# Expert second stage sub-tile by sub-tile, slot table ahead of the tile table, first dummy adds left out

## What is computed

```
x = x + 0.5 * ffn(layernorm(x)); x = x + attn(layernorm(x)); x = x + 0.5 * ffn(layernorm(x))

ffn (T = 8192 tokens, 8 experts, 2 of them a token, cap = 2560 rows an expert, F = 1024):
logits = clip(xf @ Wr); top_v, top_i = top_k(logits, 2); top_p = softmax of the two
pos = rank of a token among those of its expert; kept = pos < cap
xe = rows of xf gathered by expert and rank
h = silu(xe @ W1) * (xe @ W3); ye = h @ W2
out[token] += top_p * kept * ye
```

## Time and profile before

| | us |
|---|---|
| timed runs, median of 3 | 3054.07 |
| timed runs, lowest and highest | 3050.84, 3055.57 |
| profiled execution, its time | 3048.99 |
| profiled execution, its span | 3047.3 |
| TensorE busy | 2854.6 (94%) |
| DVE busy | 1602.6 (53%) |
| ACT busy | 1253.7 (41%) |
| POOL busy | 1158.8 (38%) |

### The profile page before, as it was taken

One profiled execution on the slowest core, in us unless ns is written; L12 is line 12 of the kernel. 1 busy time (PEld: TensorE's weight loads), 2 busy tenths in 40 slices (PEclk: granted clock), 3 DMA queues, 4 the chain that ended last, 5 costly groups with the idle time before them and its releaser, 6 DMA issues. The chain is left out here.

```text
span 3047.3 us, 54514 instructions
## 1 busy us (share of the span) xinstructions
PE 2854.6 (94%) x18727; PEld 2543.1 (83%) x18727; DVE 1602.6 (53%) x3791; ACT 1253.7 (41%) x2685; POOL 1158.8 (38%) x1560
## 2 busy tenths in 40 slices
PE   5379999999999999979999994999999999999997
PEld 3368898989899988868888884898998998898986
DVE  8843544454454545347778775345545454445443
ACT  5233434344444434334444442344434343444433
POOL 3654444444443434310111123443434443444432
PEclk9689999999999999989999996999999999999999
DMA  7542323232323312220111013323323232323221
GB/s 251 177 119 39 80 36 77 42 77 42 77 44 75 84 30 41 36 54 29 58 56 59 30 44 95 85 40 76 77 43 77 42 81 32 80 42 77 41 36 26
DMA packets 156550, 198.51 MB, mean 65 GB/s; under 512 B 15696, under 2 KB 128464, under 8 KB 156368
## 3 DMA queue, kind: packets, MB, share of 16 engines
q0 software_dynamic: 64128, 88.42, 17.6%
q1 hardware_dynamic: 81952, 97.30, 9.8%
q10 hardware_dynamic: 10288, 10.38, 1.0%
HBM read 124.32 MB, written 80.11 MB: 67 GB/s over the span
## 5 line engine op out<-in xcount | busy, mean ns | idle before, releaser
L1259 DVE TENSOR_TENSOR e_h_lo<-e_hid,e_h_hi 128x384 fp32r<-128x384 f32 (+1 forms) x640 | 383.7, 600 | 399.2 <-ACT e_h_hi L1219 399.2
L1256 DVE TENSOR_TENSOR e_hid<-e_ps,e_gate 128x384 f32<-128x384 f32 (+1 forms) x640 | 382.0, 597 | 308.4 <-ACT e_gate L1215 308.3
L1219 ACT ACTIVATE e_h_hi<-e_hid 128x384 fp32r<-128x384 f32 (+1 forms) x640 | 356.7, 557 | 444.1 <-DVE e_hid L1256 443.8
L1215 ACT ACTIVATE e_gate<-e_ps 128x384 f32<-128x384 f32 (+1 forms) x640 | 333.5, 521 | 330.7 <-PE e_ps L101 330.5
L99 PE MATMUL e_ps<-e_xT_hi,c_wa 128*128 128x384 f32 (+1 forms) x1280 | 454.5, 355 | 9.0 <-DVE e_yrow L1269 6.0
L99 PE MATMUL e_ps<-e_xT_hi,e_wb 128*128 128x384 f32 (+1 forms) x1280 | 460.3, 360 | 0.0
L100 PE MATMUL e_ps<-e_xT_lo,e_wb 128*128 128x384 f32 (+1 forms) x1280 | 455.1, 356 | 0.0
L101 PE MATMUL e_ps<-e_xT_hi,e_wb 128*128 128x384 f32 (+1 forms) x1280 | 455.0, 355 | 0.0
L101 PE MATMUL e_ps<-e_xT_hi,c_wa 128*128 128x384 f32 (+1 forms) x1280 | 449.7, 351 | 0.0
L100 PE MATMUL e_ps<-e_xT_lo,c_wa 128*128 128x384 f32 (+1 forms) x1280 | 449.7, 351 | 0.0
L433 POOL DMA_INDIRECT c_xrow<-normed_rows,e_token x320 | 347.8, 1087 | 156.6 <-issue 91.3
(11 more groups left out here) (297 smaller groups left out, 5189.5 us busy)
## 6 DMA issues: line engine op xcount, KB each, us to landing
c_raw<-w SPq DMA_DIRECT2D x204, 256.0 KB, 5.5
normed_rows<-r_xn SPq DMA_DIRECT2D x8, 1056.0 KB, 7.2
normed_rows<-mi_xn SPq DMA_DIRECT2D x8, 1056.0 KB, 4.7
x<-x ACTq DMA_DIRECT2D x8, 1024.0 KB, 12.3
out<-mi_x SPq DMA_DIRECT2D x8, 1024.0 KB, 5.3
r_xin<-x SPq DMA_DIRECT2D x7, 1024.0 KB, 11.0
c_raw<-x SPq DMA_DIRECT2D x7, 1024.0 KB, 8.1
c_xrow<-normed_rows,e_token POOLq DMA_INDIRECT x320
```

The costliest lines, as they stand in the source:

```text
L1215: act.activation(gate[:, f % 2, 0:n], ps1[f % 2][:, 0:n], ACT.Silu).then_inc(gated, 1)
L1219: act.activation(h[0][:, f, 0:n], hid[:, f % 2, 0:n], ACT.Copy).then_inc(h_high, 1)
L1256: dve.tensor_tensor(hid[:, f % 2, 0:n], ps3[f % 2][:, 0:n], gate[:, f % 2, 0:n], ALU.mult).then_inc(hid_ready, 1)
L1259: dve.tensor_tensor(h[1][:, f, 0:n], hid[:, f % 2, 0:n], h[0][:, f, 0:n].bitcast(F32), ALU.subtract).then_inc(h_ready, 1)
```

## The change

1. `Router.tiles` is cut in two: `read_counts` (its first instruction, which frees the PSUM bank) stays where it was, and `read_table` now goes ahead of the rest, in the route phase ahead of `low_w` too.
2. The second stage on TensorE runs by sub-tile: 0 and 2 for f = 0 to 6, both for f = 7, then 3 (in a big tile), then 1. `y_made` and `y_kept` go up at each sub-tile, ACT and DVE take the sub-tiles in that order, and `y_lent_kept` is gone: slice 1 of the next tile waits for all but the last sub-tile of this one.
3. On POOL `meta(g + 1)` goes behind the adds of iteration g and ahead of its gather, and waits for the landing of those adds. The first expert's first tile sends no adds (its code is written out in front of the loop), and the single dummy add is gone.
4. The last tile's adds are issued one by one as their sub-tiles are kept.
5. The first turn of a phase takes three sub-tiles instead of four, and the two splits of x behind it 384 columns instead of 512.
6. The loads of x1's groups 1 and 2 go from the end of e1_ to SP's start in the middle phase.

```diff
-    def tiles(self, dve, table):
+    def read_counts(self, dve):
+        dve.wait_ge(self.count_made, 1)
+        dve.tensor_scalar(self.lg[:, 0, :], self.rank_bank[...], float(CAP), float(P - 1), ALU.min, ALU.add)
...
-                r.tiles(dve, tiles_out)
+                r.read_counts(dve)
+                dve.wait_ge(r.tabled, T // P // QUAD)
+                r.read_table(dve, r.table_bank[:, 0:SCOLS], slot_token)
                 for q in range(LOW_BY_POOL, PIECES):
                     low_w(q)
-                dve.wait_ge(r.tabled, T // P // QUAD)
-                r.read_table(dve, r.table_bank[:, 0:SCOLS], slot_token)
+                r.tiles(dve, tiles_out)
...
-                def tile(e, subs, at, behind, g):
-                    meta(g)
+                def tile(e, subs, at, behind, g, adds=True):
                     hold(e, subs, at, g)
-                    wait_alone(pool, y_kept, g + 1, k.passed)
-                    add(BIG)
+                    if adds:
+                        wait_alone(pool, y_kept, BIG * g + BIG, k.passed)
+                        add(range(BIG))
+                    meta(g + 1, adds)
                     gather(behind, g)
...
-                wait_alone(pool, held, 1, k.passed)
-                add(1)
-                with pool.Fori(0, E) as e:
+                meta(0, False)
+                expert(0, adds=False)
+                with pool.Fori(1, E) as e:
                     expert(e)
...
-                wait_alone(pool, y_kept, n + 2, k.passed)
-                add(SMALL)
+                for sub, kept in zip(RESULTS[SMALL], (1, BIG - 1, BIG)):
+                    wait_alone(pool, y_kept, BIG * n + BIG + kept, k.passed)
+                    add((sub,))
...
                         if f == 1:
-                            pe.wait_ge(y_lent_kept, g + 1)
+                            pe.wait_ge(y_kept, BIG * g + 2 * BIG - 1)
...
+                    for f in range(KF - 1):
+                        second(f, 2)
+                    pe.wait_ge(h_ready, KF * g + KF)
+                    for sub in (0, 2):
+                        second(KF - 1, sub).then_inc(y_made, 1)
...
-        for g in (1, 2):
-            sp.dma_start(x1[:, g], x1_g[g]).then_inc(self.x_loaded[g], 16)
...
+                load(1)
+                load(2)
                 for g in range(MGS):
```

More of the change, by code:

```diff
@@ L44 @@
 MAX_BIG, MAX_SMALL, MAX_TILES = 3, 4, 6
+RESULTS = {SMALL: (0, 2, 1), BIG: (0, 2, 3, 1)}
 TAIL = 2 * BIG
@@ L377, in count @@
         pe.matmul(self.rank_bank[:, self.RANK_AT:self.RANK_AT + E], self.k.ones[:], self.seen[:], start=True, stop=True).then_inc(self.count_made, 1)
+    def read_counts(self, dve):
+        dve.wait_ge(self.count_made, 1)
+        dve.tensor_scalar(self.lg[:, 0, :], self.rank_bank[:, self.RANK_AT:self.RANK_AT + E], float(CAP), float(P - 1),
+                          ALU.min, ALU.add).then_inc(self.count_read, 1)
     def tiles(self, dve, table):
@@ L385, in tiles @@
         scan, zero, count = self.lg[:, 2, :], self.lg[:, 3, :], self.lg[:, 4, :]
-        dve.wait_ge(self.count_made, 1)
-        dve.tensor_scalar(units, self.rank_bank[:, self.RANK_AT:self.RANK_AT + E], float(CAP), float(P - 1), ALU.min,
-                          ALU.add).then_inc(self.count_read, 1)
         dve.memset(zero, 0.0)
@@ L1058, in add @@
                 def add(subs):
-                    for sub in range(subs):
+                    for sub in subs:
                         pool.indirect_dma_start(
@@ L1063, in add, with meta @@
                             compute_op=ALU.add).then_inc(y_added, 16)
-                def meta(g):
-                    pool.wait_ge(y_added, WORDS * g + 16)
+                def meta(g, adds):
+                    if adds:
+                        pool.wait_ge(y_added, WORDS * g - WORDS)
                     wait_alone(pool, held, g + 1, k.passed)
@@ L1141, in _, with turn @@
                 pe.nop().then_inc(y_made, 1)
-                def turn(n_loaded):
+                def turn(n_loaded, subs=BIG):
                     pe.wait_ge(x_loaded, n_loaded)
                     for half in range(KD):
-                        for sub in range(BIG):
+                        for sub in range(subs):
                             ins = pe.transpose(psx[:, half, sub * P:(sub + 1) * P],
@@ L1156, in wt, with second @@
                         return both[:, 0, at:at + P], both[:, 1, at:at + P]
-                    def second(f, of):
+                    def second(f, sub):
                         at = W2AT + f * D
-                        for sub in of:
-                            own, bank = slice(sub * P, (sub + 1) * P), ybank[sub]
-                            pe.matmul(bank[:].rearrange("p (u d) -> p u d", u=2), h[0][:, f, own],
-                                      both[:, :, at:at + D], start=(f == 0), stop=False)
-                            ins = pe.matmul(bank[:, D:2 * D], h[1][:, f, own], both[:, 0, at:at + D],
-                                            start=False, stop=(f == KF - 1))
-                        return ins
+                        own, bank = slice(sub * P, (sub + 1) * P), ybank[sub]
+                        pe.matmul(bank[:].rearrange("p (u d) -> p u d", u=2), h[0][:, f, own],
+                                  both[:, :, at:at + D], start=(f == 0), stop=False)
+                        return pe.matmul(bank[:, D:2 * D], h[1][:, f, own], both[:, 0, at:at + D],
+                                         start=False, stop=(f == KF - 1))
                     if first:
@@ L1266, in tile @@
                             low_w(e, s, q)
-                    for i, sub in enumerate(reversed(range(subs))):
+                    for i, sub in enumerate(RESULTS[subs]):
                         dve.wait_ge(y_scaled, BIG * g + i + 1)
```

65 lines of the change are left out of this document (31 added, 34 removed).

## The result

| | before | after |
|---|---|---|
| timed runs, median (4 runs each) | 3054.82 us | 3001.07 us |
| lowest and highest | 3050.84, 3055.69 | 2999.50, 3001.51 |
| profiled execution, its time | 3048.99 | 2999.50 |
| profiled execution, its span | 3047.3 | 2997.8 |

The ratio is 0.9826, with a 95% interval of 0.9809 to 0.9843. The two profiled executions are 49.5 us apart. The other 4.3 lie in the base: the profiled execution of before was 5.8 us faster than the median of its runs, that of after 1.6. In the later experiments before had medians of 3051.6 to 3052.3 us, and beside 3051.63 the unchanged after took 3000.85, 50.8 less; the first four runs of before were somewhat slow.

What follows compares the result with a forecast made beforehand. TensorE was taken as short of work only at the expert phases' starts and the seams between phases. Terms 12.2 + 9.1 + 1.4 + 3.4 + 2.5 + 6.8 + 1.4 = 36.8 us off 3054.07 gave 3017, range 3009 to 3031.

Steps and rivals of the forecast that it cites:

- The starts: Stalls at the first tiles of both expert phases vanish: 9.1 us in the first, 12.2 in the second; first turns add 1.4.
- The seam from the middle phase: Ahead of the second expert phase, DVE's tile table runs while POOL issues the gather, saving 3.4 us.
- No stretch below a granted clock of 1.00: Sign of being right: at the first expert phase's start, no granted clock below 1 in 200 to 220 us.
- no pair slower: Second-stage matmul pairs on TensorE keep 0.346 us each; slower pairs would have shown the one-bank rival.
- Rivals (a) to (d): Tile 0 waits for dummy adds (0.12); one-bank pairs slow (0.04); landing binds every tile (0.03); dummies not holding gather (0.03).
- The first turn: In both expert phases, six transposes for eight and narrower copies save 0.7 us each, 1.4 together.
- The step that failed: In steady tiles, finishing results earlier gains 0 for the next tile's slice 1, since no steady tile waited there.
- The first seam: From routing to the first expert phase, earlier slot table, weight loads and gather save 2.5 us, bounds 1.2 and 4.0.
- SP ends last then: At the first seam SP's weight loads end last, at 155.2, 1.2 us sooner, hiding the table of tiles.
- The gather beside DVE's splits: At the first seam the gather's issue may take up to 1.4 us longer beside DVE's splits, under SP's cover.
- The ends: At both expert phases' ends, adding sub-tiles singly saves 3.9 us less some waits between adds: 3.4 each, 6.8 together.
- x1's loads: At the seam to the middle phase, SP issues two x1 loads less before the barrier, saving 1.4 us.

Runs made afterwards that it cites:

- run 8: The kernel after, with SP's twelve loads of the second expert's weights moved behind the barrier into the first expert phase; 2997.29 us, ratio 0.9823.
- run 2: The kernel before with only POOL's part (part 3) of the change, the last three adds still together; 3028.42 us, ratio 0.9928.
- run 3: The kernel before with only read_counts, the slot table first and x1's two loads behind the barrier; 3043.19 us, ratio 0.9974.
- run 5: The kernel after with two useless ACT copies ahead of the first gate of each expert's first tile; 3006.33 us.
- run 9: The kernel after with two useless DVE instructions behind the last addition of every expert tile; 3000.91 us.

## Why the prediction was wrong, point by point

**Right in mechanism and size.** The starts: 22.7 us forecast with the first turns, 22.6 measured, and POOL came in time by its own count (gather 6.4 us behind the start, forecast 5 to 7; `meta(2)` at 25.2, forecast 27 to 31; ACT's scaling started 3.0 us behind it). The seam from the middle phase: 3.5 for 3.4. No stretch below a granted clock of 1.00 from 188 to 220 us, no pair slower, and no landing wait that TensorE saw. Rivals (a) to (d) all fell. The first turn with three sub-tiles has no run of its own; from its start to the first matmul it takes 2.77 us in both phases of after, where it took 3.44 and 3.43, so 0.67 each for the 0.7 of the forecast.

**The step that failed** is "The finished results no longer matter for slice 1 of the next tile, where no steady tile waited anyway: gain 0". It asked whether TensorE waits for the results, and the row on TensorE's matmuls said no. But the engines that finish the results are also those that start the next tile, and at an expert start they have no slack. The wait stood on another row, that of the weight loads on `hid`: they wait first, and the matmul behind them then shows no idle time. 10.5 of the 12.7 us by which the sum was short are this term.

**The first seam** was sized at 2.5 with bounds of 1.2 and 4.0, and measured 4.85 from the last `tabulate` to the turn. The step that was wrong is "SP ends last then": the sum took SP's 1.2 us and bounded the rest by the barrier. SP's end had as little to do with it as in x1's case below. The new phase waits for the gather's landing (run 8). Its issue ended 6.61 us sooner and its landing took 5.2 us instead of 4.6, together 6.0, and 1.3 of these are that the routing itself ended sooner in this run. That is also the other 1.3 us of the 6.1 in the ledger, and it varies: TensorE's last `tabulate` came at 140.6 to 143.6 over the 14 traces, at 141.3 to 141.9 in the five with the old tables.

**The gather beside DVE's splits.** Its first two parts took 1.35 and 1.24 us. The first took 1.29 in before too, with no split beside it, and the second 1.02, so the gather is 0.28 us longer (in all nine traces of the new order), a fifth of the 1.4 allowed for. The sign is that of the Trainium skill (SBUF — State Buffer, "Who interferes with whom"). It was not under SP's cover, since POOL is the last into this barrier.

**The ends.** The last add came 3.95 us sooner, forecast 3.4. The missing half is the wait allowed for between the adds; there was none. The way from the last add to the next phase became 0.6 us shorter in both phases by the edit on POOL (run 2), which nobody forecast. It is POOL's DRAIN at the phase's end: 5.54 us in the traces with the old POOL code, 4.89 in those with the new, with every add landed before it starts. Why it takes as long, and why part 3 shortened it, stays open.

**x1's loads**, 1.4 forecast, 0 measured (run 3). The step counted SP's issue as the last thing ahead of the barrier, since it stood last in the rows. In after SP ends 1.4 us sooner and the barrier takes 3.37 us behind it instead of 2.57: the phase end hung on POOL, whose DRAIN ends 2.2 us behind SP's in before and 2.9 in after.

**The middle phase** lost 2.4 us that no edit put there. The windows view, 10 us each, from the phase's start; before:

```profile
1336.00:1346.00 10.00, 5.61 (x26) 4.52 (x26) 5.65 (x31) 2.92 (x9) 1.45 (x3) 0.75 0.61 202
1346.00:1356.00 10.00, 8.80 (x84) 6.98 (x88) 2.53 (x5) 4.17 (x15) 0.00 (x0) 1.00 0.01 2
```

and after:

```profile
1310.00:1320.00 10.00, 6.54 (x26) 5.30 (x26) 5.66 (x31) 2.36 (x8) 1.45 (x3) 0.63 0.68 218
1320.00:1330.00 10.00, 8.38 (x59) 7.17 (x58) 2.49 (x4) 3.21 (x10) 0.00 (x0) 0.83 0.01 2
```

The same 26 matmuls at first, but in before the clock rises to 1.00 4.8 us behind the phase's start and stays; in after it rises at 7.0 us, is back at 0.50 from 10.4 to 13.8, and stays only then (0.83 in the second stretch for 1.00). Most of this is chance: from the start of this phase to its first scores (`mi_sc`) it took 12.7 us in the first profile of before, 14.8 in the second, and 13.1 to 15.7 in the other traces. But x1's loads now stand in this phase, and a small cost of that is not excluded: to the counts of the routing it took 509.7 to 511.7 us in the five traces with these loads ahead of the barrier (mean 510.9) and 510.4 to 513.1 in the nine with them behind it (mean 511.8). The profiled execution of before was the shortest of all. That explains some 2 us of the base too: the sum was taken off the median of 3054.07, and the profiled execution, 5 us under it, was no typical one.

## What to carry to other kernels

A steady tile that never waits says nothing about the first tile of a group, where engines do extra work: read the intervals tile by tile, and for TensorE read the waits of its weight loads as well as of its matmuls. When an edit makes a helping engine finish sooner, ask what that engine starts next, and whether it has slack there; and work that isn't urgent (here the splits of the next weights) goes a few steps behind such a late start, so that it can be made good. An instruction that stands last in the rows ahead of a barrier need not be what the barrier waits for; read the DRAIN rows of each engine's own instruction stream, which the timeline leaves out.

## What the runs showed of the hardware

- Reading three loop counts from SBUF holds up an engine's instruction stream. On DVE the three loads of 0.30 us begin 0.63 to 0.66 us apart, the first 0.11 us behind the start of the last instruction that had to wait, and the next instruction starts 2.07 to 2.11 us behind that start, though the one before it takes 0.48 (before, 14 places). On ACT, copies that wait for nothing start 1.85 us behind the start of the last scaling, 1.38 of them idle (run 5). Instructions put ahead of the reads run in that time: 0.75 us of them at each of 80 tiles added 0.5 us to the 14 expert starts together (run 9).
- At the end of a block POOL's DRAIN ends 0.20 to 0.22 us behind the landing of its last gather (28 seams in 14 traces) and POOL goes on 0.25 us later. The landing comes 1.7 to 1.9 us behind the end of the issue, but 4.6 to 5.8 beside twelve weight loads of 256 KB. SP's loads themselves are not waited for: the last one lands at 159.95 in after, where POOL starts at 155.58. With all its adds landed the DRAIN still takes 4.9 or 5.5 us.
- The clock rises from 1.2 to 2.4 GHz 4.8 to 8.1 us behind the start of the lightly loaded middle phase, over 14 traces with the same instructions there at first, and in 11 of them it falls once more before the first scores; these come after 12.7 to 15.7 us.
